# Conv-attention hybrid on one core: the third chunk's depthwise taps on ScalarE and GpSimd, the others in PSUM, skip rows outside the ring, step items a row up

## What is computed

```python
# layer 0: a scan block (both directions) and a local gate
xn = rmsnorm(x) * norm_w
u, z = split(xn @ in_proj_w.T)                        # 384 + 384 channels
u = silu(causal_conv(u, 4 taps) + conv1d_b)           # once forward, once over the flipped tokens
dt, B, C = split(u @ x_proj_w.T, [24, 40])
delta = softplus(dt @ dt_proj_w.T + dt_proj_b)
h[t] = exp(delta * A) * h[t-1] + delta * u * B[t]     # 16 states of each channel
y = sum_n(h * C) + u * D ;  out = (y * silu(z)) @ out_proj_w.T
local = sigmoid(depthwise_3x3(xn, dw_w) + dw_b) * xn
x = x + res_scale * ((fwd + bwd) * scale_mod + local)
# layer 1: layernorm, causal attention (6 heads of 64), projection, residual;
# layernorm, MLP 384-1536-384 with factored weights, gelu, residual
```

## Time and profile before

| | us |
|---|---|
| median of 3 runs | 4495.2 (4494.16 to 4502.44) |
| the profiled execution | 4498.51 |
| its span, first to last instruction | 4496.7 |
| VectorE busy | 3683.6 (82%) |
| TensorE matmuls busy | 3404.1 (76%) |
| GpSimd busy | 2574.1 (57%) |
| ScalarE busy | 2492.4 (55%) |

### The profile page before, as it was taken

The page is one execution under the profiler, slowest core; times in us unless marked ns, Lnnn a source line. Parts: engine busy times, 40 slices in busy tenths (PEclk is TensorE's granted clock), DMA queues, the critical chain, the costliest instruction groups (busy, mean ns, idle before and its releaser), DMA issues.

```text
span 4496.7 us, 40326 instructions
## 1 busy us (share of the span) xinstructions
PE 3404.1 (76%) x11626; PEld 1727.4 (38%) x11626; DVE 3683.6 (82%) x2793; ACT 2492.4 (55%) x3491; POOL 2574.1 (57%) x1628
## 2 busy tenths in 40 slices
PE   6400688878788787877878787887878778886897
PEld 2100235523364234632356233642346323551472
DVE  5999787899789997899888997899978998889221
ACT  3533456665565655656566645756556555656262
POOL 1889375674656565574756746565655746567000
PEclk9755899988899888988999888998989888997998
DMA  3999596887868887787978878688877879779100
GB/s 92 221 243 243 119 227 155 193 197 184 189 160 203 198 191 173 173 201 177 226 162 194 195 178 193 164 196 195 198 172 171 201 174 221 160 178 208 38 6 14
DMA packets 224022, 785.09 MB, mean 175 GB/s; under 512 B 25292, under 2 KB 40958, under 8 KB 223518
## 3 DMA queue, kind: packets, MB, share of 16 engines
q0 software_dynamic: 117504, 427.87, 49.5%
q1 hardware_dynamic: 106270, 354.32, 24.7%
HBM read 339.60 MB, written 39.85 MB: 84 GB/s over the span
## 4 chain that ended last, share of the span: by engine, by line
PE 45%; DVE 23%; issue 13%; DMA 7%; ACT 7%; POOL 4%; DVEq 0%; ACTq 0%; SPq 0%; POOLq 0%
DVE pBC L1154 13%; PE pW L646 9%; PE pW L565 9%; DMA y<-hb 7%; PE pW L455 7%; PE pW L498 6%; PE pW L475 4%; PE pW L532 3%; POOL hb L1331 3%; ACT pt L948 2%; PE pW L581 2%; PE pW L703 1%; DVE hb L1122 1%; DVE hb L1163 1%; PE pW L544 1%
## 5 line engine op out<-in xcount | busy, mean ns | idle before, releaser
L1154 DVE TENSOR_TENSOR_SCAN pBC<-pBC,hb 128x1024 f32<-128x1024 f32 x768 | 1757.0, 2288 | 132.5 <-ACT pBC L792 74.0
L1345 POOL DMA_DIRECT2D y<-hb x792 | 756.1, 958 | 955.9 <-DVE hb L1163 897.3
L1331 POOL TENSOR_TENSOR hb<-du_f,b_row 128x1024 f32<-128x1024 f32 x384 | 1015.6, 2652 | 71.1 <-DMA y<-hb 51.9
L1331 POOL TENSOR_TENSOR hb<-uc_b,b_row 128x1024 f32<-128x1024 f32 x384 | 993.3, 2588 | 75.1 <-DMA y<-hb 70.0
L1163 DVE TENSOR_TENSOR hb<-pBC,c_row 128x1024 f32<-128x1024 f32 x768 | 940.0, 1224 | 46.5 <-DVE pBC L1154 2.7
L792 ACT ACTIVATE pBC<-delta,vec 128x1024 f32<-128x1024 f32 x384 | 429.8, 1120 | 341.5 <-DVE hb L1163 341.5
L792 ACT ACTIVATE pBC<-xres,vec 128x1024 f32<-128x1024 f32 x384 | 429.8, 1120 | 322.8 <-DVE hb L1163 322.0
L646 PE MATMUL pW<-area,pt 128*128 128x64 f32 x3456 | 448.4, 285 | 138.0 <-ACT pt L948 138.0
L646 PEld LDWEIGHTS pW<-area,pt 128*128 128x128 f32 x3456 | 419.4, 198 | 192.7 <-ACT pt L948 184.4
L1198 DVE TENSOR_REDUCE stat<-pW 128x1 f32<-128x640 f32 (+7 forms) x361 | 258.5, 752 | 264.2 <-PE pW L568 264.2
L475 PE MATMUL pW<-area,xn_area 128*128 128x512 f32 x576 | 289.4, 661 | 96.8 <-DVE xa L1146 53.4
(11 more groups left out here) (166 smaller groups left out, 4796.1 us busy)
## 6 DMA issues: line engine op xcount, KB each, us to landing
y<-hb POOLq DMA_DIRECT2D x792, 512.0 KB, 7.0
b_row<-bc_rows SPq DMA_DIRECT2D x256, 512.0 KB, 6.2
c_row<-bc_rows SPq DMA_DIRECT2D x256, 512.0 KB, 5.3
du_f<-in_x SPq DMA_DIRECT2D x8, 1536.0 KB, 13.1
kept_residual<-in_x SPq DMA_DIRECT2D x8, 1536.0 KB, 13.9
xres<-kept_residual SPq DMA_DIRECT2D x8, 1536.0 KB, 10.8
out_x<-xa SPq DMA_DIRECT2D x8, 1536.0 KB, 6.9
kept_residual<-hb POOLq DMA_DIRECT2D x16, 512.0 KB, 5.3
```

Source lines behind the costliest of these rows:

```text
L1154: dve.tensor_tensor_scan(flow(d, buf), flow(d, buf), flow(d, hb[slot(r)][:, :]), 0.0, ALU.mult, ALU.add).then_inc(scan_done, 1)
L1331: pool.tensor_tensor(hb[q % NHB][:, :], du[d][:, k, :], b_row[g % 2][:, :], ALU.mult)\
L1345: pool.dma_start(y[:, k, :], hb[q % NHB][:, :], accum_op=ALU.add).then_inc(y_in[k], 16)
```

## The change

VectorE's `depthwise` covers chunks 0 and 1 only (18 steps) and sums them in the PSUM pairs `pBC`; `taps` names the places and `gate` where `local` writes. Chunk 2's nine taps are formed by ScalarE (`tap_row_of`, the first with the bias into `prob`, the others into `hb[1]` and `hb[2]` in turn), spread ahead of the six silus by `TAPS`, and summed by GpSimd (`depthwise`, eight additions). The three sigmoids stand together, and so do the three softplus chunks. `gated` comes before the three `local`s, and the first two step sizes on TensorE wait for `local` to have read `pBC`.

The skip rows go to their own place (`skip_row`, in `area1`) and are added by `sum_skip` behind rows 21 to 23; the ring holds scan rows only. The z projection and the convolution use other banks of `pW`, with other waits. Most items of `STEPS`, the first layernorm and `finish` 4 and 5 are a row earlier; the projections have a list of rows of their own (`PROJ`, 15 to 31), and `step_silu`, `step_x`, the skip rows and the step sizes stand behind `PLAN`'s items of their row (`BEHIND`). Attention runs in rows 33 to 60. GpSimd's clearing of the second padded query is at `scores` 1, not 0.

The diff, shortened (indents halved; left out are the semaphore names, waits that follow from the new banks, and places where `slot(r)` becomes `r % NHB`):

```diff
@@ -39,6 +39,7 @@
+TAPS = (0, 3, 4, 6, 7, 9, 9)
@@ -61,15 +62,16 @@
-RS = 24
-STEPS = ([("step_y", 2, 0)] + [("step_z", n, (5, 7, 8)[n]) for n in range(3)]
-+ [("conv", i, (9, 10, 12, 13, 14, 15)[i]) for i in range(6)]
-+ [("step_u", i, (11, 12, 14, 15, 16, 17)[i]) for i in range(6)]
-+ [("step_silu", 0, 18), ("step_x", 0, 20), ("step_bc", 0, 22)] + [("step_skip", k, RS - KT + k) for k in range(KT)]
-+ [(kind, k, 23 + 3 * k + i) for k in range(KT)
-  for kind, i in (("step_in", 0), ("step_abs", 1), ("step_log", 2), ("step_sum", 2), ("step_copy", 2))])
-FINISH = [("finish", t, (0, 0, 1, 1, 3, 3)[t]) for t in range(6)]
-Q0, S0, S1 = 15, 32, 62
+RS = 21
+STEPS = ([("step_y", 2, 0)] + [("step_z", n, (4, 6, 7)[n]) for n in range(3)]
++ [("conv", i, (8, 9, 11, 12, 13, 14)[i]) for i in range(6)]
++ [("step_u", i, (10, 11, 13, 14, 15, 16)[i]) for i in range(6)] + [("step_bc", 0, 21)])
+BEHIND = ([("step_silu", 0, 17), ("step_x", 0, 19)] + [("step_skip", k, RS - KT + k) for k in range(KT)]
+ + [(kind, k, 22 + 3 * k + i) for k in range(KT)
+  for kind, i in (("step_in", 0), ("step_abs", 1), ("step_log", 2), ("step_sum", 2), ("step_copy", 2))])
+FINISH = [("finish", t, (0, 0, 1, 1, 2, 2)[t]) for t in range(6)]
+S0, S1 = 33, 62
+PROJ = (15, 16, 17, 18, 19, 21, 22, 22, 23, 24, 24, 25, 26, 26, 27, 28, 29, 30, 31, 31)
@@ -90,18 +92,18 @@
-  norm(0, 8, 10, 11, 13, 14) + [("proj", t, Q0 + t * (S0 - 1 - Q0) // NPJ) for t in range(NPJ)] + attention()
+  norm(0, 7, 9, 10, 12, 13) + [("proj", t, PROJ[t]) for t in range(NPJ)] + attention()
-SLOTS = [[(kind, n) for kind, n, row in STEPS + FINISH + PLAN if row == r] for r in range(ROWS)]
+SLOTS = [[(kind, n) for kind, n, row in STEPS + FINISH + PLAN + BEHIND if row == r] for r in range(ROWS)]
-STEP = tuple({kind for kind, _, _ in STEPS})
+STEP = tuple({kind for kind, _, _ in STEPS + BEHIND})
@@ -178,9 +180,11 @@
-    gate = [prob[:, :], hb[4][:, :], hb[3][:, :]]
+    gate = [hb[4][:, :], hb[3][:, :], prob[:, :]]
+    tap_row = [hb[1], hb[2]]
+    skip_row = [area1[:, k * L:(k + 1) * L] for k in range(KT)]
@@ -200,6 +204,7 @@
+    taps = [pBC[0][:, :], pBC[1][:, :], gate[2]]
...
@@ -298,9 +303,9 @@
-    def slot(r):
-  return (r + (KT if r >= RS else 0)) % NHB
+    def landed(r):
+  return 16 * (r // KT + 1 + (r >= RS))
@@ -466,11 +471,10 @@
-      elif t >= 8:
+      elif t >= 6:
-      elif t >= 6:
-        pe.wait_ge(xa_ready, at(6, b - 1, t - 1))
-      bank = pW[:, t % 4 if t >= 6 else 2 + t % 2, :]
+        pe.wait_ge(xa_ready, at(6, b - 1, t - 3))
+      bank = pW[:, (t + 2) % 4 if t >= 6 else 2 + t % 2, :]
@@ -484,18 +488,19 @@
+          pe.wait_ge(r_evac, at(2, b - 1, 0))
+          pe.wait_ge(ip_evac, at(12, b, 6))
+        elif i < 4:
-        if i < 4:
-          pe.wait_ge(ip_evac, at(12, b, min(5 + i, 6)))
-        pe.wait_ge(ip_evac, at(12, b, 11 + i))
+        pe.wait_ge(ip_evac, at(12, b, 9 + i))
-        mm = pe.matmul(pW[:, 2 + i % 2 if d else (i + 2) % 4, :], cd[m][:, 128 * j:128 * j + 128],
+        mm = pe.matmul(pW[:, 2 + i % 2 if d else (i + 3) % 4, :], cd[m][:, 128 * j:128 * j + 128],
@@ -538,6 +543,8 @@
+    if g < VK:
+      pe.wait_ge(loc_ready, at(KT, b, g + 1))
...
@@ -832,8 +839,30 @@
-      act.wait_ge(dw_step, at(9 * KT, b, 9 * (k + 1)))
-      act.activation(gate[k], gate[k], ACT.Sigmoid).then_inc(sig_ready, 1)
+      if k < VK:
+        act.wait_ge(dw_step, at(9 * VK, b, 9 * (k + 1)))
+      else:
+        act.wait_ge(tap_added, at(8, b, 8))
+      act.activation(taps[k], taps[k], ACT.Sigmoid).then_inc(sig_ready, 1)
+  def tap_row_of(b, lo, hi):
+    for j in range(lo, hi):
+      win = xnp[:, VK, j // 3:j // 3 + HH, j % 3:j % 3 + WW]
+      w = vec[:, VK, V_DW + j:V_DW + j + 1]
+      if j == 0:
+        act.wait_ge(xn_ready, at(3, b, 3))
+        act.wait_ge(pad_zero, at(6, b, 6))
+        act.wait_ge(xr_step, at(5, b - 1, 0))
+        act.activation(gate[VK].rearrange("p (h w) -> p h w", w=WW), win, ACT.Identity, scale=w,
+               bias=vec[:, VK, V_DWB:V_DWB + 1]).then_inc(tap_ready, 1)
+      else:
+        if j < 3:
+          act.wait_ge(y_in[3 - j], at(YIN, b, -16))
+        else:
+          act.wait_ge(tap_added, at(8, b, j - 2))
+        act.activation(tap_row[j % 2].rearrange("p (h w) -> p h w", w=WW), win, ACT.Identity,
+               scale=w).then_inc(tap_ready, 1)
@@ -844,8 +873,8 @@
-      act.wait_ge(y_in[(RS + k - NHB) % KT], at(YIN, b, 16 * ((RS + k - NHB) // KT + 1)))
-      act.activation(hb[(RS + k) % NHB][:, :], uc[1][:, k, :], ACT.Identity, scale=dcol).then_inc(yd_ready, 1)
+      act.wait_ge(cv_ready, at(12, b, 12))
+      act.activation(skip_row[k], uc[1][:, k, :], ACT.Identity, scale=dcol).then_inc(yd_ready, 1)
@@ -918,6 +947,9 @@
+      if n == 14 and not alone(b):
+        for k in range(KT):
+          act.wait_ge(y_in[k], at(YIN, b, 16 * (RS // KT + 1)))
@@ -1010,19 +1042,15 @@
+        tap_row_of(b, TAPS[i], TAPS[i + 1])
-      gates(b, 0, 2)
+      gates(b, 0, 3)
-      for k in range(2):
+      for k in range(KT):
-      gates(b, 2, 3)
-      act.preload_act_table_set(LOG_EXP)
-      soft_abs(b, 0, 2)
-      soft_exp(b, 0, 2)
-      soft_log(b, 0, 2)
@@ -1101,33 +1129,32 @@
-  def depthwise(b, lo, hi):
-    for step in range(lo, hi):
-      k, j = step // 9, step % 9
+  def depthwise(b, k):
+    for j in range(9):
+      step = 9 * k + j
-      acc = gate[k].rearrange("p (h w) -> p h w", w=WW)
+      acc = taps[k].rearrange("p (h w) -> p h w", w=WW)
-        if k == 0:
-          dve.wait_ge(xr_step, at(5, b - 1, 0))
-        else:
-          for i in range(KT):
-            dve.wait_ge(y_in[i], at(YIN, b, 0))
+        dve.wait_ge(m2_done, at(ROWS, b, k - 1))
-        dve.wait_ge(dw_step, at(9 * KT, b, step))
+        dve.wait_ge(dw_step, at(9 * VK, b, step))
-    acc = gate[k].rearrange("p (h w) -> p h w", w=WW)
-    dve.scalar_tensor_tensor(out=acc, in0=acc, scalar=rs_col, in1=xnp[:, k, 1:1 + HH, 1:1 + WW],
-                op0=ALU.mult, op1=ALU.mult).then_inc(loc_ready, 1)
+    for i in range(KT):
+      dve.wait_ge(y_in[i], at(YIN, b, 0))
+    dve.scalar_tensor_tensor(out=gate[k].rearrange("p (h w) -> p h w", w=WW),
+                in0=taps[k].rearrange("p (h w) -> p h w", w=WW), scalar=rs_col,
+                in1=xnp[:, k, 1:1 + HH, 1:1 + WW], op0=ALU.mult, op1=ALU.mult)\
+     .then_inc(loc_ready, 1)
...
@@ -1248,18 +1275,15 @@
-      depthwise(b, 0, 20)
-      local(b, 0)
-      depthwise(b, 20, 22)
-      local(b, 1)
-      depthwise(b, 22, 27)
+      depthwise(b, 0)
+      depthwise(b, 1)
+        local(b, k)
+      for k in range(KT):
-        if k == 0:
-          local(b, 2)
@@ -1304,7 +1328,7 @@
-    elif (kind, n) == ("scores", 0):
+    elif (kind, n) == ("scores", 1):
@@ -1312,11 +1336,16 @@
-  def row_of(q):
-    return q if q < RS else q - KT if q >= RS + KT else None
-  def input_row(b, q, r):
+  def depthwise(b):
+    pool.wait_ge(tap_ready, at(9, b, 1))
+    for j in range(1, 9):
+      pool.wait_ge(tap_ready, at(9, b, j + 1))
+      if j > 1:
+        pool.wait_ge(tap_added, at(8, b, j - 1))
+      pool.tensor_tensor(gate[VK], gate[VK], tap_row[j % 2][:, :], ALU.add).then_inc(tap_added, 1)
+  def input_row(b, r):
@@ -1324,43 +1353,47 @@
-    if q in (3, 4):
-      pool.wait_ge(kept_add[5 - q], at(16, b, 16))
-    if q >= NHB:
-      pool.wait_ge(y_in[(q - NHB) % KT], at(YIN, b, 16 * ((q - NHB) // KT + 1)))
-    pool.tensor_tensor(hb[q % NHB][:, :], du[d][:, k, :], b_row[g % 2][:, :], ALU.mult)\
+    if r in (3, 4):
+      pool.wait_ge(kept_add[4 - r], at(16, b, 16))
+    if r >= NHB:
+      pool.wait_ge(y_in[(r - NHB) % KT], at(YIN, b, landed(r - NHB)))
+    pool.tensor_tensor(hb[r % NHB][:, :], du[d][:, k, :], b_row[g % 2][:, :], ALU.mult)\
-  def sum_row(b, q):
-    k, r = q % KT, row_of(q)
-    if r is None:
-      pool.wait_ge(yd_ready, at(6, b, 4 + q - RS))
-    else:
-      pool.wait_ge(m2_done, at(ROWS, b, r + 1))
-    if q < KT:
+  def sum_row(b, r):
+    k = r % KT
+    pool.wait_ge(m2_done, at(ROWS, b, r + 1))
+    if r < KT:
-      pool.wait_ge(y_in[k], at(YIN, b, 16 * (q // KT)))
-    pool.dma_start(y[:, k, :], hb[q % NHB][:, :], accum_op=ALU.add).then_inc(y_in[k], 16)
+      pool.wait_ge(y_in[k], at(YIN, b, landed(r) - 16))
+    pool.dma_start(y[:, k, :], hb[r % NHB][:, :], accum_op=ALU.add).then_inc(y_in[k], 16)
+  def sum_skip(b, k):
+    pool.wait_ge(yd_ready, at(6, b, 4 + k))
+    pool.wait_ge(y_in[k], at(YIN, b, landed(RS - KT + k)))
+    pool.dma_start(y[:, k, :], skip_row[k], accum_op=ALU.add).then_inc(y_in[k], 16)
+      depthwise(b)
-      for q in range(ROWS + KT):
-        r = row_of(q)
-        if r is not None:
-          for kind, i in beside(r, layer1, more):
-            item(kind, i, b, more)
-          input_row(b, q, r)
-        if q >= LAG:
-          sum_row(b, q - LAG)
-      for q in range(ROWS + KT - LAG, ROWS + KT):
-        sum_row(b, q)
+      for r in range(ROWS):
+        for kind, i in beside(r, layer1, more):
+          item(kind, i, b, more)
```

(7 more changed lines are left out.)

## The result

| | before | changed kernel |
|---|---|---|
| median of the runs, us | 4494.7 (4491.4 to 4502.4, 4 runs) | 4301.6 (4299.0 to 4303.5, 4 runs) |
| profiled execution / its span, us | 4498.5 / 4496.7 | 4300.2 / 4298.4 |
| VectorE busy, us (share) | | 3586.2 (83%) |
| TensorE's granted clock, mean | 0.862 | 0.874 |

The ratio is 0.957 [0.955, 0.958]: faster, 193 us less, where 212 had been forecast (4283, range 4240 to 4345).

The account below looks back on a forecast made before the run. VectorE's work was taken to bound the boundary between samples, and waits for other engines rows 15 to 32. Gains of 62.6, 106 and 43 us sum to 212, off the profiled 4498.5; median 4283 us, range 4240 to 4345.

Parts of the forecast that it names:

- Part 1: Boundary between samples: one of VectorE's three chunks of taps moves to other engines; 62.6 us less (45 to 75).
- X + 21.7: Boundary: the last du ends 21.7 us after the last silu's start (X); first scan 8.6 us earlier.
- Sample 1: Boundary of sample 1: the additions push the last silu by 2.7 us, so the gain is 5.2 us.
- Rival (b): Boundary: additions end 4 to 5 us too late for the third gate, gain 4 not 8.6; 4313 us; chance 0.15.
- the slower rival (c): Boundary: GpSimd's eight additions take 7 us each, delaying the third gate and first scan; 4527 us; chance 0.02.
- Part 2: Rows 15 to 32: waits for decay, GpSimd and softplus shrink; 106 us less (60 to 150).
- 13 a sample: Rows 15 to 32: waits kept in the sum, 13 us a sample, where the hand sum found 9.
- rival (d): Rows 15 to 32: hand sum of 9 us of waits is right, 4 us more in seven samples; 4245; chance 0.15.
- wrong: landings over 3 us in GpSimd's queue: Rows 21 to 25: GpSimd's queue waiting over 3 us for y landings, the scan behind them, would show the forecast wrong.
- Part 3: First attention scores of a sample and rows 47 and 48: 6.1 us in seven samples, 43 us less (10 to 50).
- The first scores: First two attention rows: last step size ready two rows ahead, so 2.2 us of 1.45 and 1.44 goes.
- The seam: Rows behind the empty attention slot in row 46: waits of 5.36 and 1.07 us become ordinary, 3.9 us gained.

Follow-up runs that it names:

- the taps alone: Only the boundary change (two chunks of taps in PSUM on VectorE, the third on ScalarE and GpSimd) put into the kernel before: 4446.1 us, ratio 0.989.
- the kernel with the empty slot: Changed kernel with attention from row 32, 28 slots over 30 rows, so row 46 has no attention slot again: 4359.1 us, ratio 0.969.

## Why the prediction was right, point by point

**What bounds the kernel** was right for rows 15 to 32, where the waits went, and nearly so for the boundary: it is shorter by VectorE's work, but the chain that is then last still holds VectorE up to local 0.

**Part 1: the mechanism was right, its size wasn't: 50.1 for 62.6.**
- First tap, 0.4 us more: measured 0.53 more (1344 against 812 ns). The upper end of my bounds was too low: a single-input pass with PSUM out took 1344 ns, one with PSUM in and out 1290. The Trainium skill (VectorE: DVE Perf Modes, "Why PSUM operands drop a tier") has an fp32 operand in PSUM lose the two-port mode; the direction agrees with 812 to 1344 ns. It wasn't free: the step size waits for local 0, and the two first taps are 1.1 us of what stands ahead of it without a gap.
- Accumulating taps +-0: right, 1290 ns.
- The term that failed is X + 21.7. Samples 2 to 7 have 24.1 on average (23.7 with the taps alone). 1.3 of the 2.4 us is the first abs at X + 10.8 instead of 9.5, 0.6 the chunks 3.41 apart. Both come from TensorE: its wait for local 0, a term that the sum didn't have, and the lower clock behind it. Where that stop is filled the abs is at X + 9.9 and the chunks 3.1 apart, and where local 0 comes early as well at X + 9.5. The rest is the last du, beside GpSimd's product. I had seen that du at 3.47 us in the earlier trace rows and still took "up to 0.4". And even with the first two at their forecast values the scan would have stood until X + 23.0 in sample 4 for the B row (X + 20.6 and a product of 2.35), a third chain that the sum left out; in the kernel with the taps alone it is that chain, or its collision with the last du, that makes 23.7 in most samples. In return, and by luck as far as the sum goes, 1.3 us were gained ahead of X (row 95 to X: 29.4 before, 28.1 after), which the forecast had only as a bound. 8.6 forecast, 7.5 measured.
- Sample 1: 5.2 forecast, nothing measured. The chain of additions pushes the last silu by 4.6 us behind the silu of z, not 2.7. GpSimd's additions come 2.67 us apart there: 0.14 us lies between two of them, and the first two take 3.1 us beside the gated product, which VectorE now does at the same time (5.65 us for three, 3.49 where it stands alone). And X to the scan is 24.3, not 21.7, by the lower clock of the small projection.
- The moved taps hide in samples 2 to 7: the additions take 2.36 us and come 2.5 apart, the third and fourth 2.5 to 3.5, and the last ends 0.4 to 1.0 us behind X, well ahead of the third gate at X + 3.8 to 4.7; nothing waits for it. Rival (b) and the slower rival (c) didn't come. (c) put its point at 6.5 us an addition; 2.5 to 3.5 was measured, from one to the next.

**Part 2: right, 109.9 us of waiting gone for 106 forecast,** and of the "13 a sample" that I kept, samples 1 to 7 hold 11.5 in rows 12 to 34 (9.5 to 14.0; the first scores come on top). But the split wasn't right everywhere: GpSimd's waits are 3.8 us on average, not 2 to 3, and of sample 4's softplus waits 5.7 us were to stay, and 9.2 did (7.8 before), while other samples lost theirs (sample 3: 10.6 before, 3.9 after). One decay wait stayed at 2.87, not 1.5. Taking 13 over the hand sum of 9 was the better choice by a little, and rival (d) fell with it. The sign "wrong: landings over 3 us in GpSimd's queue" did appear:

```profile
2118.80 0.86 POOL L1377 DMA_DIRECT2D y<-area  x1 [3.04 <-DMA y<-hb]
...
2128.89 0.87 POOL L1377 DMA_DIRECT2D y<-area  x1 [1.60 <-DMA y<-hb]
2139.09 0.88 POOL L1371 DMA_DIRECT2D y<-hb  x1 [3.72 <-DMA y<-area]
```

That is 8.4 us in GpSimd's queue in sample 4, of which the scan felt 1.9 (2 to 3 forecast). GpSimd's waits over the run missed their mark all the same (33.7 against "under 25"), the decay's met it (21.1, under 30).

**Part 3: near in sum, 36.1 us of waiting gone for 43, but not by its two terms.** The first scores gave 0.2 us a sample, not 2.2: the 1.45 and 1.44 of sample 4 are 1.90 and 1.50 after. That step failed: having the last step size two rows ahead of them didn't end the wait. The last projection lies two rows ahead of the first scores in both kernels, and with one row between (the kernel with the empty slot) their waits grew; that points to the projections, but no run moves them alone. The seam gave 5.0 us of waiting, not 3.9, which is the 6.43 less two ordinary waits; the attention slot that I took off besides is only moved. That these two errors, and those within part 2, cancel to 148.3 for 149 is in part luck.

**The signs.** First scan after row 95's addition: 46.6 us in sample 4 (44 forecast, 52.9 before). No tap beyond 1.3: right for the accumulating ones (1.29 at most), missed for the first taps (1.34). Score waits down by 40: 36. Seam: right.

## What to carry to other kernels

When work leaves the engine that bounds a boundary, list every chain that ends at the next instruction, the loads too, and price each to its end: here two ended within a microsecond of one another (X + 24.0 and X + 23.0 in sample 4), and the second (small projection, store, broadcast load, product) was not in the sum. A price for a pass beside another engine is taken from the row that shows the two together; and when a wait of such a neighbour is removed, look at what it will run beside next. Where parts of a stage are bound by several small waits, keeping a part of them in the sum (here half) came closer than the hand sum of those that have a name. A sum that comes out right can hide terms that don't: check each against its own rows, as the first scores and the seam show here.

## What the runs showed of the hardware

- A tensor_scalar with a padded SBUF window in and PSUM out took 1344 ns for 1024 columns of f32, 812 with SBUF out; a scalar_tensor_tensor in the same place took 1290 and 1285.
- Both engines pay when VectorE and GpSimd each read two SBUF operands: VectorE 1290 to 1996 ns, GpSimd 2381 to 2869, averaged over the run; 1.22 to 3.63 us for a single du. With one VectorE operand in PSUM neither pays (1290 and 2381 ns).
- TensorE's granted clock fell from 1.00 to 0.57 behind a stop of 1.75 us that followed a stretch with 5.4 of 7.9 us busy; with one matmul more and a stop of 0.41 us at that place it was 0.82 over the next 9.3 us. That brought the step sizes forward, and the first scan by less than a microsecond.
- Behind a stop of 4.44 us it was 0.68 over the next 7.8 us, and a small-projection matmul took 1.06 us, then 0.59.
